# Attention sums of probabilities: ones as the stationary operand in four tiles of 32 columns, reciprocals taken on rows of 256 columns, eight small DMAs that put the queries back on partitions

## The reference

```python
x = x + attention(layernorm(x))        # then a routed FFN, a state-space layer, a second FFN

Q = einsum('btd,hkd->bthk', x, W_Q) + b_Q      # K and V alike
scores = einsum('bqhk,bshk->bhqs', Q, K) / sqrt(64)
attn = softmax(scores, axis=-1)
out_h = einsum('bhqs,bshk->bqhk', attn, V)
return einsum('bqhk,hdk->bqd', out_h, W_O) + b_O
```

## Time and profile before

| | |
|---|---|
| time, median of 3 runs | 1141.75 us (lowest 1139.01) |
| time of the profiled execution | 1148.81 us |
| its span in the trace | 1147.5 us |
| PE busy | 1091.5 us, 95% |
| DVE / ACT / POOL busy | 827.9 / 617.2 / 761.0 us |
| attention | about the first 717 us of the span |

### The profile page before, as it was taken

One profiled execution on the slowest core, in us unless ns is written; L12 is line 12 of the kernel. 1 busy time (PEld: TensorE's weight loads), 2 busy tenths in 40 slices (PEclk: granted clock), 3 DMA queues, 4 the chain that ended last, 5 costly groups with the idle time before them and its releaser, 6 DMA issues.

```text
span 1147.5 us, 19727 instructions
## 1 busy us (share of the span) xinstructions
PE 1091.5 (95%) x7578; PEld 676.4 (59%) x7578; DVE 827.9 (72%) x1226; ACT 617.2 (54%) x866; POOL 761.0 (66%) x394
## 2 busy tenths in 40 slices
PE   7999999999999999999999999959789988899998
PEld 4565665665665655666665566858444434445786
DVE  6875776675765775676876547325889999997987
ACT  4453544553544554543453444436986565857753
POOL 5688788788787797777789750320589797995200
PEclk9999999999999999999999999989899999999999
DMA  6000000000000000000000233456464444441000
GB/s 208 1 2 1 1 2 1 1 2 2 1 2 1 1 2 1 2 1 1 2 6 15 91 112 104 127 183 206 146 215 146 149 146 147 139 155 37 10 10 19
DMA packets 38093, 68.86 MB, mean 60 GB/s; under 512 B 5968, under 2 KB 24144, under 8 KB 38000
## 3 DMA queue, kind: packets, MB, share of 16 engines
q1 hardware_dynamic: 34992, 64.52, 17.7%
q0 software_dynamic: 1024, 2.10, 0.6%
q10 hardware_dynamic: 1984, 0.98, 0.3%
HBM read 61.30 MB, written 6.16 MB: 59 GB/s over the span
## 4 chain that ended last, share of the span: by engine, by line
PE 79%; issue 7%; DVE 5%; POOL 4%; ACT 3%; DMA 1%; another core or an unknown queue 1%; POOLq 0%; SPq 0%; DVEq 0%; ACTq 0%
PE psum L651 20%; PE psum L612 16%; PE psum L637 6%; PE psum L625 5%; PE psum L669 5%; PE psum L1019 3%; PE psum L925 3%; PE psum L1002 3%; POOL hc L2181 3%; PE psum L717 2%; PE psum L703 2%; PE psum L684 2%; PE psum L783 2%; PE psum L794 2%; DVE psum L1852 1%
## 5 line engine op out<-in xcount | busy, mean ns | idle before, releaser
L2093 POOL TENSOR_TENSOR psums<-psums,prob 128x1024 f32<-128x1024 f32 x180 | 427.8, 2376 | 26.1 <-POOL psums L2093 0.5
L1568 DVE TENSOR_REDUCE mx<-psum 128x2 f32<-128x1024 f32 x256 | 301.3, 1226 | 127.3 <-PE psum L637 126.4
L1118 ACT ACTIVATE prob<-psum 128x1024 f32<-128x1024 f32 x256 | 261.4, 1027 | 66.5 <-PE psum L625 38.6
L651 PE MATMUL psum<-prob,V 128*64 128x512 f32 x1024 | 243.7, 598 | 0.0
L2181 POOL TENSOR_TENSOR hc<-hs,cc 128x1024 f32<-128x1024 f32 x64 | 151.6, 2369 | 21.0 <-DVE hs L1859 18.5
L1859 DVE TENSOR_TENSOR_SCAN hs<-dA,psum 128x1024 f32<-128x1024 f32 x64 | 146.3, 2287 | 2.2
L2093 POOL TENSOR_TENSOR psums<-prob 128x1024 f32<-128x1024 f32 x30 | 72.2, 2406 | 106.7 <-ACT prob L1118 106.7
L1127 ACT COPY oraw<-psum 128x512 f32<-128x512 f32 x32 | 18.8, 587 | 210.4 <-PE psum L651 210.4
L925 PE MATMUL psum<-hc,ident 128*128 128x512 f32 x256 | 122.8, 602 | 2.5 <-DVE slot_rows_h L1867 1.4
L651 PEld LDWEIGHTS psum<-prob,V 128*64 128x64 f32 x1024 | 66.6, 137 | 97.5 <-issue 93.7
L612 PE MATMUL psum<-q_hi,k_hi 64*128 64x512 f32 x512 | 106.8, 405 | 2.6 <-ACT prob L1118 2.5
(11 more groups left out here) (294 smaller groups left out, 1709.7 us busy)
## 6 DMA issues: line engine op xcount, KB each, us to landing
cc<-C_rows SPq DMA_DIRECT2D x64, 512.0 KB, 3.7
kq_wts<-in_e_rows SPq DMA_DIRECT2D x14, 578.0 KB, 4.3
e_wts<-in_e_rows SPq DMA_DIRECT2D x10, 578.0 KB, 3.9
e_w<-in_e_rows SPq DMA_DIRECT2D x6, 578.0 KB, 4.0
slots_in<-e_zero SPq DMA_DIRECT2D x2, 960.0 KB, 7.1
slots_out<-e_y SPq DMA_DIRECT2D x30, 64.0 KB, 2.1
e_w<-in_e_w SPq DMA_DIRECT2D x1, 1024.0 KB, 7.3
slot_rows_h<-slots_in SPq DMA_DIRECT2D x3, 256.0 KB
```

The costliest lines, as they stand in the source:

```text
L651: ins = pe.matmul(A.O[HALF[s], :], A.V[pair % 2][:, j, s * DH:(s + 1) * DH], A.prob[unit(pair, c, j) % NPB][:, s * CH:(s + 1) * CH], start ...
L1118: act.activation(A.prob[n % NPB][:, :], slots.bank("score", pair, c, j).rearrange("p s n -> p (s n)"), ACT.Exp, scale=float(DH) ** -0.5).t ...
L1568: dve.tensor_reduce(K.A.mx[:, :, t, c], slots.bank("max", pair, t, c), AXX, ALU.max).then_inc(*slots.inc("max", pair, t, c))
L2093: pool.tensor_tensor(total[:, :], (K.A.prob[(n - 1) % NPB] if j == 1 else total)[:, :], K.A.prob[n % NPB][:, :], ALU.add).then_inc(*K.psum ...
```

## The change

For pairs 0 to 14 the roles in `sumhalf` are swapped: 32 columns of ones are stationary, and 256 columns of `A.psums[c]` move, in four matmuls that go to the four groups of 32 output partitions of one bank. Each of these partitions then holds the same 256 sums in a row. The reciprocal is taken on 128x256 values into a new buffer `A.inv_rows[c]`. SP gets a new step, `sp_inverse`: after the reciprocal it issues eight DMAs, each from one row of 128 values (512 bytes on one partition) to one column of `A.inv` (4 bytes on each of 128 partitions). `dve_out` waits for these DMAs instead of the reciprocal. The columns of `A.inv` are numbered anew. The last pair keeps the 16 matmuls of before.

```diff
 def pe_sum_half(K, pe, pair, c):
     A, bank = K.A, K.work.bank("sumhalf", pair, c)
     pe.wait_ge(*added(K, pair, c, NT - 1))
     pe.wait_ge(*K.work.free("sumhalf", pair, c))
+    if pair < LAST:
+        for i in range(4):
+            ins = pe.matmul(bank[32 * i:32 * i + 32, 0:2 * P], A.ones[:, :], A.psums[c][:, 2 * P * i:2 * P * (i + 1)], start=True, stop=True)
+        ins.then_inc(*K.work.full.inc("sumhalf", pair, c))
+        return
     for t in range(4):
         for s in range(2):
             for half in range(2):
-                at = s * CH + t * P + half * LO
-                ins = pe.matmul(bank[HALF[half], s * NT + 4 * c + t:s * NT + 4 * c + t + 1], A.psums[c][:, at:at + LO],
-                                A.ones[:, :], start=True, stop=True)
+                at, to = s * CH + t * P + half * LO, inv_column(s, 0, t)
+                ins = pe.matmul(bank[HALF[half], to:to + 1], A.psums[c][:, at:at + LO], A.ones[:, 0:1], start=True, stop=True)
...
 def dve_sum_half(K, dve, pair, c):
...
+    A, bank = K.A, K.work.bank("sumhalf", pair, c)
     dve.wait_ge(*K.work.full.at("sumhalf", pair, c))
-    if pair:
-        dve.wait_ge(*K.slots.empty("out", pair - 1, c))
-    dve.reciprocal(half(K.A.inv[:, :]), half(K.work.bank("sumhalf", pair, c)[:, 0:2 * NT])).then_inc(*K.work.inc("sumhalf", pair, c))
+    if pair < LAST:
+        if pair:
+            dve.wait_ge(A.inv_set[c], 128 * pair)
+        dve.reciprocal(A.inv_rows[c][:, :], bank[:, 0:2 * P]).then_inc(*K.work.inc("sumhalf", pair, c))
+        return
...
 def dve_out(K, dve, pair, c):
...
-    dve.wait_ge(*K.work.empty("sumhalf", pair, c))
+    if pair < LAST:
+        dve.wait_ge(A.inv_set[c], 128 * (pair + 1))
+    else:
+        dve.wait_ge(*K.work.empty("sumhalf", pair, c))
...
+def sp_inverse(K, sp, pair, c):
+
+    A = K.A
+    if pair == LAST:
+        return
+    sp.wait_ge(*K.work.empty("sumhalf", pair, c))
+    if pair:
+        sp.wait_ge(*K.slots.empty("out", pair - 1, c))
+    for i in range(8):
+        at = 8 * c + 4 * (i % 2) + i // 2
+        sp.dma_start(A.inv[:, at:at + 1], A.inv_rows[c][32 * (i // 2):32 * (i // 2) + 1, i % 2 * P:(i % 2 + 1) * P]).then_inc(A.inv_set[c], 16)
...
-SP_STEPS = {"row": sp_row, "rows": sp_rows, "fetch": sp_fetch, "yrow": sp_yrow, "loads": sp_loads, "e1_load": sp_load_experts,
+SP_STEPS = {"row": sp_row, "sumhalf": sp_inverse, "rows": sp_rows, "fetch": sp_fetch, "yrow": sp_yrow, "loads": sp_loads, "e1_load": sp_load_experts,
```

More of the change, by code:

```diff
@@ L692, in pe_row, with inv_column @@
     pe.transpose(K.work.bank("row", *k)[:, 0:P], K.A.nmx[:, :], K.ident[:, :]).then_inc(*K.work.full.inc("row", *k))
+def inv_column(s, c, t):
+    return 8 * c + 4 * (t % 2) + 2 * s + t // 2
 def pe_sum_half(K, pe, pair, c):
@@ L1606, in dve_sum_half @@
 def dve_sum_half(K, dve, pair, c):
-    def half(t):
-        return t.rearrange("p (s t) -> p s t", s=2)[:, :, 4 * c:4 * c + 4]
+    A, bank = K.A, K.work.bank("sumhalf", pair, c)
     dve.wait_ge(*K.work.full.at("sumhalf", pair, c))
-    if pair:
-        dve.wait_ge(*K.slots.empty("out", pair - 1, c))
-    dve.reciprocal(half(K.A.inv[:, :]), half(K.work.bank("sumhalf", pair, c)[:, 0:2 * NT])).then_inc(*K.work.inc("sumhalf", pair, c))
+    if pair < LAST:
[3 more added lines that the diff above has]
+        return
+    dve.wait_ge(*K.slots.empty("out", pair - 1, c))
+    dve.reciprocal(A.inv[:, 8 * c:8 * c + 8], bank[:, 0:8]).then_inc(*K.work.inc("sumhalf", pair, c))
 def dve_out(K, dve, pair, c):
@@ L1627, in dve_out @@
             ins = dve.scalar_tensor_tensor(out=K.x[:, tile, :], in0=slots.bank("out", pair, c)[:, s, t * P:(t + 1) * P],
-                                           scalar=A.inv[:, s * NT + 4 * c + t:s * NT + 4 * c + t + 1], in1=K.x[:, tile, :],
+                                           scalar=A.inv[:, inv_column(s, c, t):inv_column(s, c, t) + 1], in1=K.x[:, tile, :],
                                            op0=ALU.mult, op1=ALU.add)
@@ L2406, in two_layer_program @@
                 K.ld[name] = (loaded, 16 * len(group))
+        A.inv_set = sems("inv_set", NC)
         A.guard_set, A.cleared, A.biased = sems("guard_set", 2), sem("cleared"), sem("biased")
@@ L2465, in two_layer_program @@
             A.bq, A.bk = sba("bq", [P, NPAIR]), sba("bk", [P, NPAIR])
-            A.bv, A.bo, A.ones = sba("bv", [P, H * DH]), sba("bo", [P, D]), sba("ones", [P, 1])
+            A.bv, A.bo, A.ones = sba("bv", [P, H * DH]), sba("bo", [P, D]), sba("ones", [P, 32])
             A.V = [sba(f"V{i}", [P, NT, 2 * DH]) for i in range(2)]
@@ L2472, in two_layer_program @@
             A.mx, A.nmx, A.mrow = sba("mx", [P, 2, NT, NC]), sba("nmx", [P, P]), sba("mrow", [P, P], F32R)
-            A.inv = sba("inv", [P, 2 * NT])
+            A.inv, A.inv_rows = sba("inv", [P, 2 * NT]), [sba(f"inv_rows{c}", [P, 2 * P]) for c in range(NC)]
             A.oraw = sba("oraw", [P, SEQ])
```

## The result

The changed kernel takes 1197.19 us in the median of four runs (1194.91 to 1200.78), the kernel before 1141.57 beside it: a ratio of 1.049, 95% interval 1.047 to 1.051. One of the four executions of the kernel before took 6167.9 us and stays out of the ratio; the other three lie at 1139.01 to 1141.75. The change costs 55.6 us, against the 66 us forecast. The profiled execution has a span of 1199.5 us, against 1147.5 before.

What follows compares the result with a forecast made beforehand. PE alone was taken to bound the attention. Pair-end waits of 51.7 us, less 3 gained, plus 2 in the last pair, made 51; 15 for the clock made 66 on 1141.75: 1208 us, range 1155 to 1245.

Steps and rivals of the forecast that it cites:

- two guard issues: SP's queue behind the eight inverse DMAs: issuing the two guard DMAs takes 1.30 us, from 8.9 to 10.2.
- from there to the guard's matmul: End of SP's last guard issue to PE's start on the guard: 1.07 us, as in pair 0.
- sums to guard: Phase c = 1, from the start of `sumhalf`: guard lands at 11.3 us, where PE needs it at 7.63.
- all 15 ends: Pair ends: each 3.67 us longer from PE's wait for the guard, less 3.3 us of cover, together 51.7 us.
- the clock: PE idle about 3.8 us at pair ends: clock halves at one end in three, 5 x 3 = 15 us.
- PE's own part: `sumhalf` on PE: 0.91 us falls to 0.7 us, a gain of 0.2 us each time.
- The reciprocal: DVE's reciprocal grows from 8 columns to 256, at 6.3 ns a column: 208 ns becomes 1.8 us.
- The issue price: SP's queue: each inverse DMA takes 0.79 us with its gap, eight take 6.3 us, ahead of the guard DMAs.
- Rival 1: SP issues inverse DMAs at 0.53 us; wait 1.6 us per end, no clock falls: +18, 1160 us; chance 0.15.
- The last pair: Reciprocals of pair 14, half 1, reach DVE late, about 693.6 against 692.7: 2 us lost.
- What hid it elsewhere: All other places: the inverse has a full phase, about 17 us, against the 10 it needs, and costs nothing.
- Rival 4: Not slower: eight issues and reciprocal both cheap, together under about 4.5 us; about 1142 us; chance 0.10.

Runs made afterwards that it cites:

- e4: Kernel before with only the four-tile sums on PE, reciprocal still on eight columns, no inverse copies, outputs not normalised rightly: 1134.26 us, ratio 0.9945.
- e6: Changed kernel with four inverse copies a half of 256 numbers each instead of eight of 128, still ahead of the guard: 1150.11 us, ratio 1.0015.
- e2: Changed kernel with the reciprocal on 8 of the 256 columns, copies still ahead of the guard, outputs not normalised: 1159.4 us, ratio 1.0159.
- e5: Changed kernel with six of the first half's eight inverse copies ahead of the next pair's guard copies, the last two behind: 1173.44 us, ratio 1.0227.
- e1: Changed kernel with the first half's eight inverse copies issued behind the next pair's two guard copies instead of ahead: 1137.07 us, ratio 0.9965.
- e7: Changed kernel with guard first; sums are copied and sent, then one reciprocal of eight columns follows their landing: 1143.27 us, ratio 0.9959.

## Why the prediction was right, and where its steps were not

The direction and the mechanism held: PE's own gain vanishes in a wait for the guard, which stands behind eight inverse DMAs in SP's queue. Of the terms:

| term, us | forecast | measured |
|---|---|---|
| sums, start to the next `pv` | 0.70 | 0.57 |
| reciprocal of 256 columns | 1.8 | 1.757 |
| eight inverse issues | 6.3 | 4.98 |
| two guard issues | 1.3 | 1.42 |
| from there to the guard's matmul | 1.07 | 1.15 |
| sums to guard | 11.3 | 10.14 |
| all 15 ends | +51.7 | +38.7 |
| the clock | +15 (5 falls) | +20 to 23 (12 falls) |

- **PE's own part** was sized well. All four tiles run side by side: 1024 columns in 0.57 us from start to start. Over the whole kernel e4 gives 0.21 us a place by the ratio and 0.24 by the medians, against 0.2 forecast. The Trainium skill, TensorEngine Tiling (Array Packing), Tiling Modes, has 128x32 as four independent tiles; the trace agrees, with eight records in 0.64 us.
- **The reciprocal**: the price of 6.3 ns a column, from two comparisons of 8-column rows, holds on 248 more columns: (1757 - 208) / 248 = 6.25 ns. The Trainium skill, VectorE: DVE Perf Modes, in the walkthrough of the 8-slice pipeline, led to an estimate of 2.1 us; the measurement decides, and the plain sum from rows was nearer.
- **The issue price** is the step that failed most in the wait: 0.79 us a copy, against 0.62. The 14 ns for each further DMA engine were read out of two forms of the guard DMA and carried from 8 to 16 engines; e6 shows a copy with twice the numbers at the same 601 ns, and it is below the guard's own 686. The nearest row was the guard's 629 itself, and no more was to be added. This made the forecast wait 1.2 us too long at each plain end, 17 us over 15; five ends came out longer than 10.14 (10.42 to 12.43) and took 4 of them back, which leaves the 13 us of the table.
- **The clock** failed the other way. From falls behind 3.73 us of idle and none behind 3.22, I took one end in three at 3.8 us. It fell at 12 of the 15 ends, with 2.52 us of idle at most of them. A fall was cheaper than assumed, since most lasted 3.4 us: 1.3 to 1.5 us each, and 2.7 where it lasted 6.8. Rival 1 had "no clock falls" at 1.6 us of waiting: behind the four idle times of 1.57 to 1.69 us in e2 and e5 there was none. The two errors, 13 us too much and 5 to 8 too little, cancel in part, and that is luck: the 1208 is nearer to 1197 than its terms deserve. Up to the end of the attention the sum is 57.4 us against 66 forecast; the 5.4 us that came back behind it stood in no term.
- **The last pair**: I put 2 us for late inverses; DVE waited 0.58 us for them. The cost lay one step earlier, at the end of pair 14, where a weight load stands between inverse and guard DMAs in SP's queue: distance 12.43 us, 4.29 more than in the earlier trace rows, PE idle for 4.3. Timeline of the changed kernel there:

```profile
723.32 5.02 SPq L2278 DMA_DIRECT2D inv<-inv_rows  x8
...
729.12 0.34 SPq L2304 DMA_DIRECT2D e_wts<-in_e_rows  x1
729.57 1.51 SPq L2264 DMA_DIRECT2D guard<-mrow  x2
...
733.26 0.80 PE L625 MATMUL psum<-guard,row_one 64*128 64x512 f32 x2 [4.30 <-DMA guard<-mrow]
```

From the last inverse issue to the first guard issue it is 1.23 us here, 0.09 at the end shown in the section on the result, and from the guard's issues to its matmul 2.18 against 1.15. I had counted the inverse DMAs there and neither the load behind them nor the slower landing; what slowed the landing is not shown.
- **What hid it elsewhere**: the inverses had a full phase to arrive in, as said; in e1 the copies of half 0 go out 1.5 us after the guard, and PE waits nowhere in the attention's pairs for their users.
- Rival 4's condition, issues and reciprocal together under 4.5 us, is confirmed by e6 from its other side: 2.40 + 1.76 = 4.16 us, and the time is that of the kernel before.

## What to carry to other kernels

In a queue that issues in order, a DMA costs its issue, here 0.6 us, to everything behind it, even if it moves 512 bytes and nobody needs it for 10 us. So before adding small DMAs, find the one in that queue which the busiest engine waits for, and put them behind it; another engine's queue helps only if that engine has slack where they stand. And a wait of one or two microseconds on TensorE should be priced with the clock that may follow it: here 38.7 us of waiting brought some 20 us more.

## What the runs showed of the hardware

- TensorE's clock fell to 1.2 GHz behind idle stretches of 1.88 to 2.32 us at 5 of 13 places, and behind those of 2.51 to 2.99 us at 10 of 12 in the changed kernel, while one of 3.22 us was not followed by a fall; ten matmuls that nobody reads, in the same 2.5 us, kept it at 2.4 GHz from 60 to 755 us. The idle length alone does not say when it falls; what else does is open.
- A copy of one row of SBUF across 128 partitions takes SP 0.60 us to issue, whether 4 or 8 bytes go to each partition, and lands about 2 us after; from ScalarE's queue it takes 622 ns.
- VectorE's reciprocal takes 6.25 ns a column, its copy 425 ns for 256 columns. To move sums and invert eight columns afterwards (0.425 + 0.19 us in e7) takes less of VectorE's time than to invert 256 and move them (1.757); the time of the whole kernel does not tell the two apart.
